# Conditioned multi-head attention: totals, sums and values of the last four steps put in another order on TensorE, with a fourth score bank

## What is computed

```python
Q, K, V = (split_heads(x @ W.T + b) for W, b in ((Wq, bq), (Wk, bk), (Wv, bv)))
tQ, tK  = (split_heads(tokens @ W.T + b) for W, b in ((Wq, bq), (Wk, bk)))
scores  = einsum('bhqd,bhkd->bhqk', Q + tQ, K + tK) / sqrt(32)
out     = einsum('bhqk,bhkd->bhqd', softmax(scores, axis=-1), V)
return x + merge_heads(out)
```

## Time and profile before

| what | us |
|---|---|
| median of 3 runs (671.38 to 673.34) | 671.43 |
| the profiled execution, its own time | 671.83 |
| span of the profiled execution | 670.0 |
| PE busy in it | 661.4 (99%) |
| DVE busy | 538.9 (80%) |
| POOL busy | 486.2 (73%) |
| ACT busy | 373.4 (56%) |

### The profile page before, as it was taken

How to read it: one execution, slowest core, us unless ns; L and a number is a source line. 1 busy time by engine, 2 the same in 40 slices (tenths; PEclk the granted TensorE clock), 3 DMA queues, 4 the chain that set the end, 5 groups by cost and what they waited for, 6 DMA issues and landing times.

```text
span 670.0 us, 10084 instructions
## 1 busy us (share of the span) xinstructions
PE 661.4 (99%) x3550; PEld 447.7 (67%) x3550; DVE 538.9 (80%) x819; ACT 373.4 (56%) x659; POOL 486.2 (73%) x202
## 2 busy tenths in 40 slices
PE   8999999999999999999999999999999999999997
PEld 6776776666776666776666676666677666675442
DVE  4676888878888878888888888887988887887886
ACT  6435565556565555565555655555555555555572
POOL 5518777788777789777779777779777778766890
PEclk9999999999999999999999999999999999999999
DMA  7943334553434554434554334554334555235401
GB/s 234 254 105 90 92 94 129 143 143 97 116 96 121 143 142 115 106 99 111 142 143 123 101 101 107 141 144 126 97 111 95 142 127 123 79 94 136 128 33 48
DMA packets 48278, 79.87 MB, mean 119 GB/s; under 512 B 9826, under 2 KB 9826, under 8 KB 48226
## 3 DMA queue, kind: packets, MB, share of 16 engines
q1 hardware_dynamic: 47700, 79.21, 44.6%
q10 hardware_dynamic: 528, 0.02, 0.0%
HBM read 19.95 MB, written 8.39 MB: 42 GB/s over the span
## 4 chain that ended last, share of the span: by engine, by line
PE 95%; DVE 2%; DMA 1%; ACT 1%; SPq 0%; issue 0%; ACTq 0%
PE bank L273 26%; PE bank L373 19%; PE bank L352 18%; PE bank L393 17%; PE bank L329 13%; DVE mf L672 1%; PE bank L401 1%; DMA Ks<-lo 1%; PE bank L424 1%; DMA cT<-condT 1%; PE bank L302 0%; ACT Pt L583 0%; DVE lo L662 0%; ACT hi L561 0%; SPq L919 0%
## 5 line engine op out<-in xcount | busy, mean ns | idle before, releaser
L583 ACT ACTIVATE Pt<-bank 128x512 f32<-128x512 f32 x512 | 299.4, 601 | 228.9 <-PE bank L373 157.3
L672 DVE TENSOR_REDUCE mf<-bank 128x1 f32<-128x512 f32 x496 | 334.1, 686 | 103.2 <-PE bank L352 102.1
L859 POOL TENSOR_TENSOR A<-A,Pt 128x2048 f32<-128x2048 f32 x59 | 270.9, 4591 | 4.6
L373 PE MATMUL bank<-Qs,Ks 98*128 98x512 f32 x496 | 201.1, 407 | 0.9 <-ACT Pt L583 0.7
L352 PE MATMUL bank<-Ks,Qs 96*128 96x512 f32 x496 | 200.4, 404 | 1.5 <-DVE mf L672 0.7
L859 POOL TENSOR_TENSOR A<-Pt 128x2048 f32<-128x2048 f32 x30 | 138.4, 4612 | 3.1 <-DVE part_sums L697 2.0
L373 PEld LDWEIGHTS bank<-Qs,Ks 98*128 98x128 f32 x496 | 93.2, 188 | 59.9 <-ACT Pt L583 39.7
L833 POOL TENSOR_TENSOR Xl<-xr,Xh 128x512 fp32r<-128x512 f32 x28 | 36.1, 1291 | 119.1 <-ACT Xh L546 119.1
L393 PE MATMUL bank<-Pt,V 128*32 128x512 f32 x1024 | 116.9, 594 | 0.0
L352 PEld LDWEIGHTS bank<-Ks,Qs 96*128 96x128 f32 x496 | 93.7, 189 | 27.5 <-DVE mf L672 5.0
L273 PE MATMUL bank<-Xl,Wh 128*128 128x512 f32 x256 | 102.6, 401 | 0.0
(11 more groups left out here) (66 smaller groups left out, 376.1 us busy)
## 6 DMA issues: line engine op xcount, KB each, us to landing
Qs<-hi SPq DMA_DIRECT2D x62, 256.0 KB, 3.6
Ks<-hi SPq DMA_DIRECT2D x62, 256.0 KB, 3.6
Qs<-lo SPq DMA_DIRECT2D x31, 256.0 KB, 4.1
Ks<-lo SPq DMA_DIRECT2D x31, 256.0 KB, 4.0
xr<-xT SPq DMA_DIRECT2D x28, 256.0 KB, 2.7
res<-xT SPq DMA_DIRECT2D x28, 256.0 KB, 2.9
outT<-ot SPq DMA_DIRECT2D x28, 256.0 KB, 3.8
Qs<-mt SPq DMA_DIRECT2D x124, 4.0 KB
```

What stands on the lines that cost most here:

```text
L373: e.matmul(st_bank(u)[:, :], k[0:98, j, kc * P:(kc + 1) * P], q[0:98, j, :], start=True, stop=True).then_inc(t_st, 1)
L583: e.activation(exponentials(g)[:, kc, j, :], st_bank(u)[:, :], ACT.Exp, scale=SCALE).then_inc(a_e, 1)
L672: e.reduce_max(to[:, 4 * j + qc:4 * j + qc + 1], MXB[u % 2][:, :], AXX).then_inc(v_mx, 1)
L859: e.tensor_tensor(sums, ex[:, 0, :, :] if kc == 1 else sums, ex[:, kc, :, :], ALU.add).then_inc(p_a, 1)
```

## The change

It touches only the last four steps. In words:

1. Totals. `END_TOTALS_AT` is gone. From step G-2 on the totals of the step two before the values' step stand inside a burst of values, after its first chunk; those of step G-3 stand at the head of the burst at slot 12 of step G-1.
2. Values. Those of step G-3 (made in step G-2) go from one burst of four chunks at slot 11 to two halves at slots 9 and 13; those of step G-2 (made in step G-1) from slot 6 to halves at 4 and 9.
3. One burst near the end: at slot 12 of step G-1 the totals of G-3, chunks 0 and 1 of the last values, and the two chunks of sums of G-2 stand together. Before, the sums stood at slot 10 and the values at slot 12, and the totals at slot 7.
4. A fourth score bank, MXB[1], from slot 11 of step G-2. The sums of step G-2 therefore go to MXB[0], and those of G-1 to the output bank of step G-3 (`sums_bank`), with waits for their readers.
5. The three chunks of sums of G-1 stand together after the last slot, then values chunks 2 and 3 (before, the first chunk of the sums stood at slot 15; that is the same place).
6. On DVE the key sums of G-3 come ahead of finishing G-4, and `add_first` ahead of finishing G-3.

```diff
-END_VALUES_AT = ((1,), (8, 14), (11,), (6,))
-END_TOTALS_AT = ((2, 9), (3, 0), (3, 7))
-END_SUMS_AT = (10, 15)
+END_VALUES_AT = ((1,), (8, 14), (9, 13), (4, 9))
+END_SUMS_AT = 12
-END_BANKS = ((1, 8, 3),)
-LAST_EARLY_AT = 12
-LAST_ORDER = ((2,), (), (3,), (2, 3))
+END_BANKS = ((1, 8, 3), (2, 11, 4))
+LAST_EARLY = (0, 1)
+LAST_ORDER = (0, 2, 3)
...
+        def sums_bank(g):
+            return MXB[0] if g == G - 2 else o_bank(G - 3)
...
                         if g == G - 1:
-                            e.wait_ge(v_f, finished(G - 3, 1))
+                            e.wait_ge(v_f, finished(G - 3, FIN))
                             e.wait_ge(v_a, 1)
                         else:
-                            e.wait_ge(v_mx, SLOTS * G)
+                            e.wait_ge(v_f, finished(G - 3, 1))
                             e.wait_ge(p_a, 3 * g + POOL_ADDS)
...
-                    if n == END_VALUES_AT[i][0]:
+                    if i < 2 and n == END_VALUES_AT[i][0]:
                         values(t - 1, range(KC) if len(END_VALUES_AT[i]) == 1 else (0, 1))
+                    elif i < 2 and n in END_VALUES_AT[i]:
+                        values(t - 1, (2, 3))
+                    elif n == END_VALUES_AT[i][0]:
+                        values(t - 1, (0,))
+                        end_totals(t - 3)
+                        values(t - 1, (1, 2, 3) if len(END_VALUES_AT[i]) == 1 else (1,))
                     elif n in END_VALUES_AT[i]:
                         values(t - 1, (2, 3))
-                    if (i, n) in END_TOTALS_AT:
-                        end_totals(G - 5 + END_TOTALS_AT.index((i, n)))
-                    if i == 3 and n == END_SUMS_AT[0]:
+                    if i == 3 and n == END_SUMS_AT:
+                        end_totals(G - 3)
+                        values(G - 1, LAST_EARLY)
                         last_sums(G - 2, (0,) + tuple(range(POOL_ADDS + 1, KC)))
-                    if i == 3 and n == END_SUMS_AT[1]:
-                        last_sums(G - 1, (0,))
-                    if i == 3 and n == LAST_EARLY_AT:
-                        values(G - 1, (0, 1))
...
+            last_sums(G - 1, LAST_ORDER)
+            values(G - 1, tuple(range(len(LAST_EARLY), KC)))
...
-            key_sums(G - 4, 0)
-            key_sums(G - 4, 1)
+            for g in (G - 4, G - 3):
+                key_sums(g, 0)
+                key_sums(g, 1)
             finish(G - 4)
-            key_sums(G - 3, 0)
-            key_sums(G - 3, 1)
+            if not ADD_FIRST:
+                add_first()
             finish(G - 3)
-            if not ADD_FIRST:
+            if ADD_FIRST:
                 add_first()
```

More of the change, by code:

```diff
@@ L423, in last_sums @@
                     for j in range(4):
-                        m = e.matmul(MXB[G - 1 - g][32 * j:32 * j + 32, :], ones[:, :],
+                        m = e.matmul(sums_bank(g)[32 * j:32 * j + 32, :], ones[:, :],
                                      added_up(g)[:, j, :] if kc == 0 else exponentials(g)[:, kc, j, :],
@@ L709, in last_sums_inverted @@
                 e.wait_ge(v_f, finished(g - 1, FIN))
-                e.transpose(rr[:, :], MXB[G - 1 - g][:, :]).then_inc(v_s, 1)
+                e.transpose(rr[:, :], sums_bank(g)[:, :]).then_inc(v_s, 1)
                 e.wait_ge(v_s, g + G - 1)
@@ L824, in vector_program @@
                 added(g)
-                if g == G - 2 and ADD_FIRST:
-                    add_first()
         def pool_program(e):
```

## The result

| | before | with the change |
|---|---|---|
| median of the runs measured beside each other, us | 671.93 (671.38 to 673.34, 6 runs) | 669.45 (668.94 to 669.75, 6 runs) |
| profiled execution, its span | 670.0 | 667.4 |
| its own time | 671.83 | 669.22 |
| PE busy | 661.4 | 659.4 |

The ratio is 0.9964 with a 95% interval of 0.9953 to 0.9976: the changed kernel is 0.36% faster, 2.4 us, and the interval reaches from 1.6 to 3.2 us. The median lies inside the forecast's own range (669.4 to 670.4), at its low edge, but with the three further runs the median of the kernel before is 671.93 and no longer 671.43, so the step is larger than the 1.6 us of the sum. That the median fell so near the predicted 669.8 is in part luck: the starting point moved up by 0.50 us, and the gain came out 0.9 us larger than the sum.

What follows compares the result with a forecast made beforehand. PE was taken as the bound, at its upper clock throughout. The walked steps from 641.40 sum to 21.28 us against 22.89, 1.6 less, so the median goes from 671.43 to 669.8; forecast 669.4 to 670.4, wider range 668.9 to 671.2.

Steps and rivals of the forecast that it cites:

- a wait for `v_ml`, first burst: PE from 641.40: 0.07 lost waiting for `v_ml`, then two chunks of values 1.85 with totals inside at 0.14.
- b four scores, c values: Slots 10 to 13 with all four banks empty, 1.15 us; then values chunks 2 and 3, 1.85 us.
- d seven scores: Slots 14, 15 and 0 to 4: four take 1.15, the other three wait for exponentials; 2.57 us in all.
- e second burst with totals: Burst of values with the totals of G-4 inside, 1.99 us, to 651.02; its DVE inputs were expected ready in time.
- f five scores, g values: Slots 5 to 9: four in 1.15, the fifth waits, 1.57 us; then values chunks 2 and 3, 1.85 us.
- The fourth bank: Score banks in the tail: with three banks in the new order, scores wait for ACT, end about 664.1, gain gone.
- Totals: Groups of totals moved into bursts: 0.54 to 0.46 in all, taken back by `v_ml` and rounding; 0.14 each inside a burst.
- 17 chunks: PE's stretch before the change: the 14.17 us beside the scores' 8.72 were said to be 17 chunks and three totals.
- Rival C: DVE's queue: a slow add or late totals of G-4 delay G-3's reciprocal and PE's joint burst; slower, 673.1; chance 0.04.
- The key sums moved on DVE cost nothing: Key sums moved earlier on DVE: no cost claimed, because DVE idles 2.00 us there.
- at its upper level (2.4 GHz) throughout: Whole span: PE busy 99%, granted clock 9 tenths or more in every slice, so the time is PE's.
- "faster" (0.27): Whole kernel: chance 0.27 of a median faster by over 0.3%, meaning under 669.4.

Runs made afterwards that it cites:

- the filler: Kernel before with eight extra matmuls on PE, results never read, behind scores where PE waits for ACT: 672.09 us, ratio 0.9997 to the kernel before.

## Why the prediction was right, and where it was short

**The bound, and the walk.** The sum stood at 21.28 us for the stretch from the totals to the end of the last sums, against 22.89. Aligned at the last maxima matmul (0.97 us), the stretch begins at 640.43 and ends at 661.65: 21.22. By its steps:

| step | walked | measured |
|---|---|---|
| a wait for `v_ml`, first burst | 0.07 + 1.99 | 0.09 + 1.99 |
| b four scores, c values | 1.15 + 1.85 | 1.12 + 1.86 |
| d seven scores | 2.57 | 2.60 |
| e second burst with totals | 1.99 | 1.91 |
| f five scores, g values | 1.57 + 1.85 | 1.62 + 1.86 |
| h three scores | 0.91 | 0.89 |
| i joint burst | 3.66 | 3.63 |
| j three scores, k last sums | 0.91 + 2.76 | 0.89 + 2.76 |

**The fourth bank** was said to be needed, with 664.1 and the gain gone without it: three banks gave a tail of 26.86, 0.20 under before, where 664.1 is 0.19 under before's 664.29.

**Totals.** I booked their move as worth 0.08 at most, taken back elsewhere. Apart they cost 0.72 in all. The sum was still right, because it set a walk of the whole new order against the measured 22.89, and in the new order the scores came out cheap whatever had made them dear. Why they got cheaper was partly mis-told: it put nearly all down to shorter starving of ACT, where a group of totals alone costs up to 0.38. Inside a burst I took 0.14 for them and 0.05 was measured, which is why e is 0.08 too long in the table. The reading that the other 14.17 us are "17 chunks" is a miscount, 15 chunks stand there; no sum used it.

**DVE.** Rival C's place was right: the reciprocal of G-3 came at 654.65 and the sums at 656.28, with 1.4 to spare, where 1.5, or 1.2 by the shared port, was said. "The key sums moved on DVE cost nothing" holds in the trace, but it was not undone alone. What the prediction did not say is that the old place of the add would have cost 0.95: in this order that part of the change is a condition of the gain, not a shift at no price.

**The step that was short** is the first: "at its upper level (2.4 GHz) throughout". That was read from one execution, in which the clock happened to hold. In about half of the executions of the kernel before the mean clock shows a fall; in the one that was profiled it stood at half for some 3.5 us behind the paced scores. With the change, which has no paced run of six in front of a burst of four chunks, no execution of 18 shows it. So the measured 2.4 us is made of 1.66 us of the tail and some 0.7 us of the clock (0.6 to 0.9: in half of the executions 1.2 by their times, or 1.70 by the one profile). This was no rival in the prediction. Its chance for "faster" (0.27) was too small for that reason, while the range held. The runs of before shown at the start (671.38, 671.43 and 673.34) already had a gap of such a size in them; their clocks are not on record.

What stays open: in one execution each of the three-bank kernel (of 10) and of the bank-only kernel (of 8) the clock was 0.997 too. In the bank-only kernel the run of six takes the same 2.70 us before the same burst of four chunks, yet 1 of 8 is few against half; what stands before that run may count too. And in the first profile of the kernel before, PE has the same 3 matmuls per us in front of the burst and the clock holds at 1.00. So the filler shows that denser work there prevents the fall, but what decides whether it comes is not settled by these runs.

## What to carry to other kernels

Count how long the banks between two engines last, and cut the bursts of other work to that length: here four banks of 0.50 us stand against halves of 1.85 us, and bank and order together gave 1.66 us where they gave 0.71 and 0.20 alone. Put small matmuls of 32 output rows inside a burst of 32-row matmuls: between the scores a group cost up to 0.38 us here, inside the burst 0.05. And look at the spread of the runs before costing a change: two levels in it can be a clock that falls in a thin stretch, and a denser order can take that away on top of what its sum says.

## What the runs showed of the hardware that was not expected

- The granted clock fell to 0.50 in the middle of a program whose PE is 99% busy by the page, for about 3.5 us (0.53, 0.50, 0.50, 0.76 in four stretches of 1 us). In the stretch before it PE counts as busy too, since the records of the paced scores last 0.50 us each (0.39 for one that does not wait); what was thin is the number of them, 3 in the stretch from 650 to 651. The first profile of the same kernel has the same 3 there and no fall.
- A DVE add with two operands in SBUF and a POOL add take turns by whole instructions: the wait was 0.30 us on DVE and 2.04 us on POOL, and it stands inside the duration of the instruction that waits.
